# Turning the x tiles before they are combined, keys and values in turns, and a new order at the end of the key jobs, in a one-core gated cross-attention kernel

## The chip, the cores and the metric

The kernel runs on one core of a Trainium2 chip. The metric is the device time of one execution in microseconds, as the median of several runs. The core has five engines with a queue each: TensorE (PE in the profile; its weight loads are PEld), VectorE (DVE), ScalarE (ACT), GpSimd (POOL) and SyncE (SP), which here issues all the DMAs. Each engine works through its queue in order, and waits on semaphores for the others. The code fixes all five orders by hand.

## The reference, cut to what matters

```python
# x: (32, 64, 512), ctx: (32, 64, 512); 32 query heads, 8 key/value heads, 128 wide; float32
def xattn(x, ctx, mask, wq, wk, wv, wo):
    q = rope(heads(layernorm(x) @ wq))            # (b, 32, 64, 128)
    k = rope(repeat4(heads(ctx @ wk)))            # 8 heads, each used by 4 query heads
    v = repeat4(heads(ctx @ wv))
    attn = softmax(q @ k.T / sqrt(128) + mask)
    return merge(attn @ v) @ wo
x = x + tanh(g_xattn) * xattn(x, ctx, ...)
# then a mixture of 8 rank-16 experts, top 1, on layernorm(x)
logits = layernorm(x) @ route_w.T
x = x + tanh(g_ffn) * lora_of_the_best_expert(...)
```

Here rope(y) is y * cos + rotate_half(y) * sin.

## The kernel before, in words

**Precision.** A float32 product is made of three products of parts: each operand is split into a high part (the value rounded to fp32r by an ACT copy) and a low part (the value less the high part, a subtraction on DVE or POOL). So one product over 128 rows is three matmuls, and every tile that comes to PE has an ACT "high" and a DVE or POOL "low" first.

**Stages.** The 2048 tokens are 4 chunks of 512. The first stage is 64 *jobs* (list `JOBS`, L67): keys of a chunk are 8 jobs (one for each head), values of a chunk are 8 jobs. A job is 12 matmuls into one of four PSUM banks (score, turned, attn0, attn1, in turn; `make`, L767), so job n may start only when DVE has read the bank of job n - 4. Then come `WIDE` = 60 and 4 more *steps* (L1240 on for DVE): each does the scores, the softmax, the values and the output projection of a quarter chunk and the projection of later queries.

**What follows a key job.** ACT copies the two halves of the bank, swapped, to a rotation buffer (`shift`, L1434), POOL multiplies it by sin (`by_sin`, L1675), DVE multiplies the bank by cos into kst (`finish_job`, L1105, `by_cos`, L1095) and adds both (`finish_key`, L1120, `rope_add`, L1100). **After a value job** ACT makes the high part and DVE the low part, in vst. Queries are treated like keys: a sum of two products (`q_sum`, L1124), shift, by_sin, by_cos, rope_add. The rotation buffers are few (`rot_slot`, L234): two, or four while x_third is free for it, and a shift waits until its buffer's last user has been added.

**The x tiles.** The queries use a 2 x 2 block scheme with 7 products in place of 8. For that, sums and differences T1 to T4 of blocks of x are needed, as they are of wq. A *pair* is two tiles of 128 tokens, c0 and c1, of 512 columns each. There are 8 pairs, and `X_BESIDE` (L101) says beside which job each is worked on. Before: the tiles are normalised (DVE, with POOL's power for 1/std), then POOL makes T1 to T4 of both tiles (`combine_x`, L1657, 4 operations of 128 x 256, into `combined`), then PE turns c0's four blocks, the eight blocks of `combined` and two of c1's, 14 transposes of 128 x 128 into the three proj banks and small (`turn_x`, L785), and ACT and DVE split these banks into xB, high and low (`x_highs`, L1391, `x_lows`, L1085). The pairs lie at jobs 8, 11, 13, 16 and 32, 35, 38, 41; combined 1 job and turned 4 jobs after that. Three places in SBUF hold the x pairs.

**The end of the jobs.** From job 47 the first weights of wq are combined (`combine_weights`, L1636) and split, from job 50 the products of the first two query blocks stand between the key jobs (`Q_AFTER`), and after job 62 PE does the scores of step 0. The last rows of every engine's job loop then run into step 0, where PE turns the probabilities after `normalise(0)` on POOL, and multiplies them with the values after `prob_low(0)` on DVE.

The functions that the change touches, with what calls them, are:

## Time and profile before

| What | us |
|---|---|
| Median of 3 runs | 1132.73 |
| Lowest, highest | 1132.55, 1134.85 |
| Profiled execution, whole | 1134.35 |
| Its span in the profile | 1132.6 |
| PE busy in it | 1103.6 |
| DVE, ACT, POOL busy | 899.3, 630.8, 619.2 |
| TensorE clock granted, mean | 0.994 |

The span is the time from the first to the last instruction on the engines; the whole execution of the profile is 1.75 us more, and is itself inside the range of the three runs. In a timeline row the first number is the start in us from the start of the span, the second the time that the row covers, and the last, in square brackets, how long the engine had been idle and on whom it had waited. A matmul's shown time reaches past the start of the next one, so the time that a group of matmuls costs is read from one start to the next.

### The profile page before, as it was taken

How to read it: one execution, taken by the hardware profiler on the slowest of the kernel's cores; microseconds unless marked ns; L12 is line 12 of the kernel's file. 1: busy time of each engine (PE TensorE's matmuls, PEld its weight loads, DVE VectorE, ACT ScalarE, POOL GpSimd, SP SyncE). 2: the span in 40 equal slices, each digit the busy share in tenths (PEclk: the TensorE clock that was granted, in tenths of full speed). 3: DMA queues.
4: the chain of work that ended last, by engine and by line, in shares of the span. 5: the costliest groups of instructions: out<-in, count | busy, mean ns of one | idle time of the engine just before them, and what ended most of it. 6: DMA issues, size and time to landing. Idle time of an engine off the chain costs nothing.

```text
span 1132.6 us, 17085 instructions
## 1 busy us (share of the span) xinstructions
PE 1103.6 (97%) x5664; PEld 923.1 (82%) x5664; DVE 899.3 (79%) x1407; ACT 630.8 (56%) x1096; POOL 619.2 (55%) x519
## 2 busy tenths in 40 slices
PE   7999999989999999999999999999999999999998
PEld 6788888768888888888888778888888888888875
DVE  6975748877877878788778999877887888778887
ACT  6453446566666666666666545455555555555443
POOL 4751458868777777777764433343444443443423
PEclk9999999989999999999999999999999999999999
DMA  6869955476464646464559735453535353533201
GB/s 221 264 235 361 340 163 214 140 270 231 139 230 148 233 145 225 147 215 160 174 189 375 263 127 169 152 177 102 190 122 197 121 187 114 177 110 105 75 1 75
DMA packets 93510, 206.27 MB, mean 182 GB/s; under 512 B 8816, under 2 KB 41712, under 8 KB 87536
## 3 DMA queue, kind: packets, MB, share of 16 engines
q1 hardware_dynamic: 93424, 205.18, 53.3%
q8 instruction: 47, 0.77, 0.3%
q14 instruction: 39, 0.32, 0.1%
HBM read 122.31 MB, written 82.84 MB: 181 GB/s over the span
## 4 chain that ended last, share of the span: by engine, by line
PE 64%; DVE 14%; POOL 10%; issue 7%; ACT 4%; DMA 0%; DVEq 0%; SPq 0%; ACTq 0%; POOLq 0%
PE attn L896 20%; PE proj L830 17%; PE score L847 7%; PE attn L782 6%; POOL rot L1680 4%; PE score L782 3%; PE turned L782 3%; POOL wq_s L1655 2%; PE attn L881 2%; PE turned L858 2%; PE attn L883 2%; DVE q_r L1140 2%; DVE q_r L1098 1%; DVE row_sum L1169 1%; DVE wo_s L1093 1%
## 5 line engine op out<-in xcount | busy, mean ns | idle before, releaser
L896 PE MATMUL attn<-wo_s,o_s 128*128 128x512 f32 x1524 | 374.6, 395 | 0.8 <-DVE o_s L1189 0.8
L830 PE MATMUL proj<-xB,wq_s 128*128 128x512 f32 x1344 | 337.1, 394 | 4.2 <-ACT copies L1466 2.2
L896 PEld LDWEIGHTS attn<-wo_s,o_s 128*128 128x128 f32 x1524 | 280.9, 188 | 57.9 <-DVE o_s L1189 1.4
L830 PEld LDWEIGHTS proj<-xB,wq_s 128*128 128x128 f32 x1344 | 252.9, 189 | 58.5 <-ACT copies L1466 2.6
L1680 POOL TENSOR_TENSOR rot<-rot,tab 128x512 f32<-128x512 f32 x112 | 170.3, 1521 | 174.2 <-ACT rot L1445 174.0
L847 PEld LDWEIGHTS score<-k_r,q_r 128*128 128x128 f32 x1024 | 124.1, 193 | 13.6 <-DVE q_r L1103 8.0
L1444 ACT ACTIVATE rot<-q_r 64x512 f32<-64x512 f32 x86 | 54.2, 630 | 143.0 <-DVE q_r L1140 138.2
L847 PE MATMUL score<-k_r,q_r 128*128 128x64 f32 x1024 | 123.5, 274 | 3.2 <-DVE q_r L1103 3.2
L1181 DVE TENSOR_TENSOR p_low<-turned,p_high 64x512 fp32r<-64x512 f32 x128 | 88.0, 688 | 40.4 <-ACT p_high L1482 38.4
L1490 ACT ACTIVATE o_s<-attn 128x512 fp32r<-128x512 f32 x127 | 69.3, 595 | 77.6 <-PE attn L883 77.6
L1103 DVE TENSOR_TENSOR q_r<-q_r,rot 128x512 f32<-128x512 f32 x86 | 89.0, 1035 | 17.0 <-POOL rot L1680 11.8
L1680 POOL TENSOR_TENSOR rot_third<-rot_third,tab 128x512 f32<-128x512 f32 x40 | 61.5, 1539 | 68.4 <-ACT rot_third L1445 68.4
L1098 DVE TENSOR_TENSOR q_r<-q_r,tab 128x512 f32<-128x512 f32 x128 | 94.0, 734 | 4.7
L1201 DVE SCALAR_TENSOR_TENSOR acc<-attn,gates_t,acc 128x512 f32<-128x512 f32 x127 | 94.6, 745 | 3.4 <-PE attn L896 1.4
L1189 DVE TENSOR_TENSOR o_s<-attn,o_s 128x512 fp32r<-128x512 f32 x127 | 81.3, 680 | 5.4 <-ACT o_s L1490 5.4
L1140 DVE TENSOR_TENSOR q_r<-copies,proj 128x512 f32<-128x512 f32 x128 | 81.6, 674 | 0.0
L1481 ACT ACTIVATE p_high<-turned 64x512 fp32r<-64x512 f32 x128 | 75.4, 589 | 6.8 <-PE turned L858 4.4
L1482 ACT ACTIVATE p_high<-turned 64x512 fp32r<-64x512 f32 x128 | 75.9, 593 | 1.5
L1466 ACT ACTIVATE copies<-proj 128x512 f32<-128x512 f32 x96 | 57.4, 598 | 27.7 <-PE proj L830 26.3
L1692 POOL TENSOR_TENSOR prob_odd<-prob_odd,row_inv 128x512 f32<-128x512 f32 x32 | 43.5, 1359 | 51.3 <-DVE row_inv L1171 51.3
L1692 POOL TENSOR_TENSOR prob_even<-prob_even,row_inv 128x512 f32<-128x512 f32 x32 | 43.2, 1349 | 46.4 <-DVE row_inv L1171 46.4
L1444 ACT ACTIVATE rot_third<-q_r 64x512 f32<-64x512 f32 x40 | 25.2, 630 | 67.6 <-DVE q_r L1140 67.2
(230 smaller groups left out, 1702.7 us busy)
## 6 DMA issues: line engine op xcount, KB each, us to landing
wq_kept<-wq_s SPq DMA_DIRECT2D x16, 1792.0 KB, 6.3
wq_s<-wq_kept SPq DMA_DIRECT2D x16, 1792.0 KB, 8.4
v_kept<-vst SPq DMA_DIRECT2D x64, 256.0 KB, 4.7
v_s<-v_kept SPq DMA_DIRECT2D x128, 128.0 KB, 4.9
wo_kept<-wo_s SPq DMA_DIRECT2D x32, 512.0 KB, 3.7
wo_s<-wo_kept SPq DMA_DIRECT2D x32, 512.0 KB, 5.3
k_kept<-kst SPq DMA_DIRECT2D x32, 256.0 KB, 2.0
wq_raw<-in_wq SPq DMA_DIRECT2D x16, 512.0 KB, 5.5
```

Source lines behind the costliest of these rows:

```text
L782: last = e.matmul(b[:, :], stationary, moving, start=(kt == 0 and m == 0), stop=(kt == KT - 1 and m == 2))
L830: last = e.matmul(dst[:, :], wq_s[:, b % 2, A, s, kt, :], xB[:, B, mv, kt, :], start=(first and kt == 0 and m == 0), stop=(kt == 1 and m = ...
L847: last = e.matmul(score[:, col:col + SEQ], two_heads, k_r[:, u % 2, seq * SEQ:(seq + 1) * SEQ], start=True, stop=True)
L896: last = e.matmul(out_bank(k, bp)[:, :], o_s[:, s, bp, h, :], wo_s[n % WO_SLOTS][:, m, :], start=(h == 0 and i == 0), stop=(h == GROUP - 1 ...
L1098: e.tensor_tensor(dst, src, cos, ALU.mult).then_inc(times_cos, 1)
L1103: e.tensor_tensor(dst, dst, by_seq(rotated(r)), ALU.add).then_inc(rope_added, 1)
L1140: e.tensor_tensor(q_tile(b, j), by_seq(copies[:, copy, :]), by_seq(proj[PRODUCTS[i][2]][:, :]), ALU.add).then_inc(q_summed, 1)
L1181: e.tensor_tensor(p_low[rows, :, twin, :], turned[rows, :].rearrange("p (b n) -> p b n", b=PAIRS), p_high[rows, twin, :].bitcast(F32).rear ...
L1189: e.tensor_tensor(low, src, high.bitcast(F32), ALU.subtract).then_inc(out_low, 1)
L1201: e.scalar_tensor_tensor(out=acc[:, tile, :], in0=out_bank(k, bp)[:, :], scalar=gates_t[:, 0:1], in1=acc[:, tile, :], op0=ALU.mult, op1=AL ...
L1680: e.tensor_tensor(r3, r3, sin, ALU.mult).then_inc(times_sin, 1)
L1692: e.tensor_tensor(by_row(k), by_row(k), row_inv[:, k % 2, :].unsqueeze(2).to_broadcast([P, ROWS, SEQ]), ALU.mult).then_inc(normalised, 1)
```

## The change

It has three parts.

1. **x is turned first.** PE turns c0 and c1 as they are: 8 transposes into two banks, 3 jobs after the pair's place in `X_BESIDE`. ACT copies the two banks back over the tiles (`x_copies`, new). POOL combines these turned tiles, and ACT and DVE split c0, `combined` and c1 from SBUF into xB, 5 jobs after the place. There are five places for x pairs, two of them in `far_raw0`. The pairs lie at jobs 8, 11, 14, 18, 34, 36, 38, 40.
2. **Keys and values of chunk 1 in turns.** Jobs 16 to 31 alternate between a key and a value job.
3. **The end of the key jobs and the first steps.** On DVE the addition of a key (`finish_key`) moves behind the next job's query sums, or to where the next job begins; the row sums of step 0 come before the last key job is finished. On POOL the weights' last combine moves from step 0 to beside the end of the jobs, half of it between `subtract_max(0)` and `normalise(0)`; the zeros of p_low move behind `normalise(0)`. On ACT the copy of step 0's middle product goes ahead of the query's shift. The four rotation buffers last until job 62, where before they ended with job 59.

```diff
-JOBS = [*keys_of(0), *values_of(0), *keys_of(1), *values_of(1), *values_of(2), *values_of(3), *keys_of(3), *keys_of(2)]
+BOTH_1 = [job for pair in zip(keys_of(1), values_of(1)) for job in pair]
+JOBS = [*keys_of(0), *values_of(0), *BOTH_1, *values_of(2), *values_of(3), *keys_of(3), *keys_of(2)]
...
-X_BESIDE = {8: 4, 11: 5, 13: 6, 16: 7, 32: 0, 35: 1, 38: 2, 41: 3}
-X_COMBINE, X_TURN, X_PLACES = 1, 4, 3
+X_BESIDE = {8: 4, 11: 5, 14: 6, 18: 7, 34: 0, 36: 1, 38: 2, 40: 3}
+X_TURN, X_COMBINE, X_SPLIT = 3, 4, 5
...
-FOUR_UNTIL, ZEROS_BESIDE = 60, 62
+FOUR_UNTIL, ZEROS_BESIDE = 63, 63
...
             def turn_x(pair):
-                c0, c1 = (x_place(w) for w in X_PAIRS[pair])
-                T = combined[:, :, :, :].rearrange("p b k n -> p (b k n)")
                 e.wait_ge(ln_done, NORM_NO[X_PAIRS[pair][1]] + 1)
-                for i in range(4):
-                    b = (proj + [small])[i]
+                for c, w in enumerate(X_PAIRS[pair]):
                     if X_NO[pair]:
-                        e.wait_ge(x_low, 4 * X_NO[pair] - 4 + i + 1)
...
+                        e.wait_ge(x_copied, 2 * X_NO[pair] - 1 + c)
+                    turn(proj[c], 0, x_place(w), cols=KT).then_inc(x_turned, 1)
...
@@ vector, the loop over the jobs
                 if n in X_BESIDE:
                     x_norms_begin(X_BESIDE[n])
+                for q in SUMS_BESIDE.get(n, ()):
+                    q_sum(*q)
+                if n > KEYS_3_MADE:
+                    finish_key(JOBS[n - 1])
+                if n > SCORES_AFTER:
+                    sum_rows(0)
+                finish_job(n)
                 if n == SCORES_AFTER:
                     mask_scores(0)
-                for q in SUMS_BESIDE.get(n, ()):
-                    q_sum(*q)
-                finish_job(n)
...
-                finish_key(JOBS[n])
-                for w in SPLITS_BESIDE.get(n, ()) if n >= KEYS_3_MADE else ():
-                    raw_low(w)
+                if n < KEYS_3_MADE:
+                    finish_key(JOBS[n])
...
-                if n - X_TURN in X_BESIDE:
-                    x_lows(X_BESIDE[n - X_TURN])
-            sum_rows(0)
+                for w in SPLITS_BESIDE.get(n, ()) if n >= KEYS_3_MADE else ():
+                    raw_low(w)
+                if n - X_SPLIT in X_BESIDE:
+                    x_lows(X_BESIDE[n - X_SPLIT])
...
@@ vector, step 0, behind its early query sums
+                if k == 0:
+                    finish_key(JOBS[-1])
...
@@ scalar
+            def x_copies(pair):
+                for c, w in enumerate(X_PAIRS[pair]):
+                    e.wait_ge(x_turned, 2 * X_NO[pair] + c + 1)
+                    e.activation(x_place(w), proj[c][:, :], ACT.Copy).then_inc(x_copied, 1)
...
             def x_highs(pair):
+                e.wait_ge(x_copied, 2 * X_NO[pair] + 2)
                 for i, (src, (high, low)) in enumerate(x_split(pair)):
-                    e.wait_ge(x_turned, 4 * X_NO[pair] + i + 1)
+                    if i in (1, 2):
+                        e.wait_ge(x_combined, 4 * X_NO[pair] + 2 + i)
...
+                for p in middle if k == 0 else ():
+                    copy_product(*p)
                 for q in ropes[0]:
                     q_shift(*q)
-                for p in middle:
+                for p in middle if k else ():
                     copy_product(*p)
...
@@ gpsimd, combine_x
-                e.wait_ge(ln_done, NORM_NO[X_PAIRS[pair][1]] + 1)
+                e.wait_ge(x_copied, 2 * no + 2)
                 if no:
-                    e.wait_ge(x_turned, 4 * no - 1)
+                    e.wait_ge(x_low, 4 * no)
...
@@ gpsimd, the loop over the jobs
-                if n == SCORES_AFTER:
-                    subtract_max(0)
...
+                if n == SCORES_AFTER:
+                    subtract_max(0)
+                    combine_weights(HEAD_PAIRS + 1, (0,))
+                    normalise(0)
+                if n == ZEROS_BESIDE:
+                    e.wait_ge(rope_added, FOUR.stop)
+                    e.memset(p_low[:, :, :, :].bitcast(F32), 0.0).then_inc(zeros_set, 1)
-            normalise(0)
+            combine_weights(HEAD_PAIRS + 1, (1,))
```

The same in the instructions. On PE, from the values of chunk 0 to the first x pair (score, turned and attn are the banks of the jobs; tab holds the identity matrix of the transposes), before:

```order
L782 MATMUL attn<-wv_s,ctxT_52 128x512 x24
L782 MATMUL score<-wv_s,ctxT_52 128x512 x12
L754 MATMUL proj<-tab,x_near 128x128 x4
L754 MATMUL proj<-tab,combined 128x128 x8
L754 MATMUL small<-tab,x_near 128x128 x2
L782 MATMUL turned<-wv_s,ctxT_52 128x512 x12
```

and in the change:

```order
L793 MATMUL attn<-wv_s,ctxT_52 128x512 x24
L765 MATMUL proj<-tab,x_near 128x128 x8
L793 MATMUL score<-wv_s,ctxT_52 128x512 x12
L793 MATMUL turned<-wv_s,ctxT_52 128x512 x12
L793 MATMUL attn<-wv_s,ctxT_52 128x512 x12
```

The first pair's transposes move from behind job 12 to ahead of it, they are 8 and no longer 14, and none reads `combined`. The other seven pairs' blocks shrink in the same way.

On DVE, around the two query sums beside job 60 (q_r_71 and q_r_72 are query tiles, kst a key tile, wo_s a weight tile), before:

```order
L1103 TENSOR_TENSOR kst<-kst,x_third 128x512
L1093 TENSOR_TENSOR wo_s_61<-raw,wo_s_61 128x512
L1098 TENSOR_TENSOR kst<-attn,tab 128x512
L1103 TENSOR_TENSOR kst<-kst,rot 128x512
L1140 TENSOR_TENSOR q_r_71<-copies,proj 128x8x64
L1140 TENSOR_TENSOR q_r_72<-copies,proj 128x8x64
L1098 TENSOR_TENSOR kst<-score,tab 128x512
L1103 TENSOR_TENSOR kst<-kst,rot 128x512
L1093 TENSOR_TENSOR wo_s_62<-raw,wo_s_62 128x512
L1098 TENSOR_TENSOR q_r_71<-q_r_71,tab 128x8x64
L1098 TENSOR_TENSOR kst<-turned,tab 128x512
L1103 TENSOR_TENSOR q_r_71<-q_r_71,rot 128x8x64
```

and in the change:

```order
L1094 TENSOR_TENSOR wo_s_61<-raw,wo_s_61 128x512
L1104 TENSOR_TENSOR kst<-kst,x_third 128x512
L1099 TENSOR_TENSOR kst<-attn,tab 128x512
L1141 TENSOR_TENSOR q_r_71<-copies,proj 128x8x64
L1141 TENSOR_TENSOR q_r_72<-copies,proj 128x8x64
L1104 TENSOR_TENSOR kst<-kst,rot 128x512
L1099 TENSOR_TENSOR kst<-score,tab 128x512
L1099 TENSOR_TENSOR q_r_71<-q_r_71,tab 128x8x64
L1094 TENSOR_TENSOR wo_s_62<-raw,wo_s_62 128x512
L1104 TENSOR_TENSOR kst<-kst,rot 128x512
L1099 TENSOR_TENSOR kst<-turned,tab 128x512
```

One addition of a key is now behind the two query sums. Between these sums and the addition to q_r_71 there are as many instructions as before, and one more key addition among them.

On POOL, from the subtraction of step 0's maximum to the second step's (prob_even and prob_odd are the probabilities of steps 0 and 1), before:

```order
L1702 MEMSET p_low 128x1024
L1687 TENSOR_TENSOR prob_even<-prob_even,neg_max 128x512
L1680 TENSOR_TENSOR rot<-rot,tab 128x512 x2
L1692 TENSOR_TENSOR prob_even<-prob_even,row_inv 128x512
L1680 TENSOR_TENSOR rot<-rot,tab 128x512
L1655 TENSOR_TENSOR wq_s<-wq_raw,wq_s 128x2x256
L1655 TENSOR_TENSOR wq_s<-wq_raw,wq_s 128x256
L1680 TENSOR_TENSOR rot<-rot,tab 128x512
L1644 TENSOR_TENSOR combined<-wq_raw 128x256
L1645 TENSOR_TENSOR combined<-wq_raw 128x256
L1648 TENSOR_TENSOR combined<-combined,wq_raw 128x256
L1650 TENSOR_TENSOR combined<-wq_raw,combined 128x256
```

and in the change:

```order
L1705 TENSOR_TENSOR prob_even<-prob_even,neg_max 128x512
L1662 TENSOR_TENSOR combined<-wq_raw 128x256
L1663 TENSOR_TENSOR combined<-wq_raw 128x256
L1710 TENSOR_TENSOR prob_even<-prob_even,row_inv 128x512
L1698 TENSOR_TENSOR rot<-rot,tab 128x512
L1740 MEMSET p_low 128x1024
L1666 TENSOR_TENSOR combined<-combined,wq_raw 128x256
L1668 TENSOR_TENSOR combined<-wq_raw,combined 128x256
L1698 TENSOR_TENSOR rot<-rot,tab 128x512
L1673 TENSOR_TENSOR wq_s<-wq_raw,wq_s 128x2x256
```

The sine product of job 63 was ahead of the normalisation and is now behind it, with the zeros of p_low behind both. The four combines no longer stand ahead of the second step's subtraction.

## Rows read from the trace of the kernel before

**Rows 1.** The page, part 1: busy time (share of the span) xinstructions

```profile
PE 1103.6 (97%) x5664; PEld 923.1 (82%) x5664; DVE 899.3 (79%) x1407; ACT 630.8 (56%) x1096; POOL 619.2 (55%) x519
```

**Rows 2.** Stretches: us, busy of each engine, PEclk, DMA share, GB/s

```profile
210.00:240.00 30.00, 23.73 (x105) 18.92 (x104) 23.09 (x31) 17.00 (x30) 21.86 (x17) 0.83 0.68 225
```

**Rows 3.** PE's waits: engine, line <- releaser: us in total, times, longest us

```profile
PE proj L830 <- ACT copies L1466: 2.2, 1, 2.2
```

**Rows 4.** PE's timeline: start us, us, what, [idle before <- releaser]

```profile
42.22 2.43 PE L782 MATMUL score<-wv_s,ctxT 128*128 128x512 f32 x9
45.49 0.96 PE L782 MATMUL score<-wv_s,ctxT 128*128 128x512 f32 x3 [0.84 <-DVE wv_s L1093]
...
48.08 1.09 PE L754 MATMUL proj<-tab,combined 128*128 128x128 f32 x8 [1.20 <-POOL combined L1670]
...
49.14 3.00 PE L782 MATMUL turned<-wv_s,ctxT 128*128 128x512 f32 x12
...
57.87 1.04 PE L754 MATMUL proj<-tab,combined 128*128 128x128 f32 x8
58.74 0.38 PE L754 MATMUL small<-tab,x_near 128*128 128x128 f32 x2
```

**Rows 5.** DVE's timeline, the first x pair normalised

```profile
41.44 0.99 DVE L1073 TENSOR_SCALAR x_near<-x_near,moments,rstd 128x512 f32<-128x512 f32 x2
```

**Rows 6.** The transposes: count, duration in ns min/median/max, first and last start

```profile
L754 PE MATMUL proj<-tab,combined x64: 272/273/329, 48.1 to 149.7; 128*128 128x128 f32 x64
```

**Rows 7.** DVE's low parts of x in the same form

```profile
L1087 DVE TENSOR_TENSOR xB<-proj,xB x24: 675/680/684, 50.7 to 151.1; 128x512 fp32r<-128x512 f32 x24
```

**Rows 8.** Stretches in the x pairs' jobs, columns as in rows 2

```profile
60.00:80.00 20.00, 20.00 (x104) 16.93 (x103) 15.44 (x27) 10.94 (x21) 12.35 (x14) 1.00 0.64 221
...
110.00:140.00 30.00, 30.00 (x154) 25.37 (x153) 22.98 (x49) 11.49 (x23) 12.79 (x18) 1.00 1.06 351
```

**Rows 9.** POOL's timeline, the last combine of the first weights

```profile
152.51 0.73 POOL L1650 TENSOR_TENSOR combined<-wq_raw,combined 128x256 f32<-128x256 f32 x1
```

**Rows 10.** ACT's timeline, the first use of that

```profile
159.62 1.16 ACT L1433 ACTIVATE wq_s<-combined 128x512 fp32r<-128x512 f32 x2
```

**Rows 11.** PE's timeline from job 54 to step 1

```profile
199.00 1.52 PE L830 MATMUL proj<-xB,wq_s 128*128 128x512 f32 x6
200.35 2.88 PE L782 MATMUL attn<-ctxT,wk_s 128*128 128x512 f32 x12
...
213.25 2.40 PE L830 MATMUL proj<-xB,wq_s 128*128 128x512 f32 x6 [1.85 <-DVE q_r L1140]
215.45 3.78 PE L782 MATMUL attn<-ctxT,wk_s 128*128 128x512 f32 x12
219.76 2.00 PE L847 MATMUL score<-k_r,q_r 128*128 128x64 f32 x16 [0.53 <-DVE q_r L1103]
...
229.45 1.69 PE L830 MATMUL proj<-xB,wq_s 128*128 128x512 f32 x6 [2.15 <-ACT copies L1466]
232.87 1.11 PE L858 MATMUL turned<-tab,prob_even 128*128 128x128 f32 x4 [1.73 <-POOL prob_even L1692]
233.64 2.91 PE L830 MATMUL proj<-xB,wq_s 128*128 128x512 f32 x6
...
246.12 0.66 PE L858 MATMUL turned<-tab,prob_odd 128*128 128x128 f32 x4 [0.74 <-POOL prob_odd L1692]
```

**Rows 12.** DVE's timeline at the end of the jobs

```profile
201.64 1.77 DVE L1103 TENSOR_TENSOR kst<-kst,rot 128x512 f32<-128x512 f32 x1 [2.70 <-POOL rot L1680]
...
211.01 0.99 DVE L1103 TENSOR_TENSOR kst<-kst,rot 128x512 f32<-128x512 f32 x1
211.92 1.27 DVE L1140 TENSOR_TENSOR q_r<-copies,proj 128x512 f32<-128x512 f32 x2
...
218.53 1.18 DVE L1103 TENSOR_TENSOR q_r<-q_r,rot 128x512 f32<-128x512 f32 x1
```

**Rows 13.** POOL's timeline, the sine of job 63

```profile
228.86 1.28 POOL L1680 TENSOR_TENSOR rot<-rot,tab 128x512 f32<-128x512 f32 x1 [1.91 <-ACT rot L1445]
```

More of the change, by code:

```diff
@@ L371, in build @@
         acc_in = [sem(f"acc_in{t}") for t in range(HALF_TILES)]
[L372 removed]
+        x_in = [sem(f"x_in{i}") for i in range(max(X_PLACE) + 1)]
         first_in = [sem(f"first_in{i}") for i in range(len(FIRST))]
@@ L513, in x_split @@
             cols = slice(tt * P, (tt + 1) * P)
[L514 to L518 removed]
+            c0, c1 = (x_place(w) for w in X_PAIRS[pair])
+            for first, n, src in ((B11, 2, c0[:, :].rearrange("p (b k t) -> p b k t", b=2, k=2)),
+                                  (T1, 2, combined[:, 0:2]), (T3, 2, combined[:, 2:4]),
+                                  (B22, 1, c1[:, 2 * P:].rearrange("p (b k t) -> p b k t", b=1, k=2))):
+                yield src, [xB[:, first:first + n, part, :, cols] for part in range(2)]
         block = stack.enter_context(nc.Block())
```

64 lines of the change are left out of this document (28 added, 36 removed).

## The prediction

> **What bounds the kernel now.** I read the page's busy times first: PE is busy 1103.6 of 1132.6 us [rows 1], so a gain is either PE work removed or one of the few PE gaps closed. Then the stretches show where the gaps are. Up to 210 us PE is full but for its start and 45 to 49 us, from 250 us on it lacks some tenths of a us in 30, and 210 to 240 us is the exception: 23.73 us busy of 30, at a mean granted clock of 0.83 [rows 2]. The table of PE's waits says the same by cause; the largest one outside the start is that for ACT's copies [rows 3]. The timelines then give each gap its place: one of 0.84 and one of 1.20 us at the first x pair [rows 4], and 1.85, 0.53, 2.15, 1.73 and 0.74 us at the end of the key jobs, 7.0 us in sum [rows 11].
>
> What the clock adds there: six matmuls at full clock take 1.35 us from start to start, 199.00 to 200.35; at 213.25 they take 2.20 and the six at 233.64 are shown with 2.91 where 1.52 is usual. A key job of 2.88 is shown with 3.78 at 215.45 [rows 11]. That is 0.85 + 0.9 + 1.4 us, and 0.7 more for the scores that follow by their later end (an estimate): 3.9 us, at the lower of the two levels (1.2 GHz), behind idle gaps. So the stretch costs 10.9 us against full speed. Nothing else in the change's reach costs anything.
>
> **Part 1, x turned first.** Removed from PE: 14 - 8 = 6 transposes in each of 8 pairs, 48. Each is shown with 0.273 us [rows 6], but they overlap: eight of them take from 57.87 to 58.74, 0.109 each [rows 4]. 48 x 0.109 = 5.2 us. PE is the bound wherever seven of the eight blocks stand (20.00 of 20 and 30.00 of 30 us busy, rows 8), so all of it counts: 7 x 0.65 = 4.6 us for these seven.
>
> The first pair gives more. From the start of job 12 to that of job 13 PE takes 42.22 to 49.14, 6.92 us: it waits 0.84 for a wv part, and then 1.20 for POOL's last combine [rows 4]. Now the transposes come ahead of job 12 and wait only for the normalisation, which ends at 42.43 [rows 5]. They end 0.87 later, 43.3. Nine matmuls (2.04) bring PE to 45.35, the last three wait for the same wv part until 45.49, and end 0.68 later, 46.2 in place of 49.14: 3.0 us. Part 1 gives 4.6 + 3.0 = 7.6 us.
>
> What it adds: ACT copies two banks in each pair, 16 copies at 0.58 [rows 10], 9.3 us on an engine that is busy 10.94 of 20 us at its fullest here [rows 8]. POOL combines after these copies rather than before the transposes; nobody on PE waits for that now but through xB. DVE's low parts are as many, but with the source in SBUF. Before, from PSUM, all 24 large ones take 0.675 to 0.684 us [rows 7]. DVE operations with both inputs in SBUF take up to 1.77 us where POOL is working at the same time [rows 12]. So a low part costs 0 to 1.09 more. At all 24, and at half of that at the 8 small ones, this is 0 to 30.5 us of DVE time. I take a quarter, 8 us, since POOL's next combine waits for these very low parts and only the sines and 1/std meet them. It is hidden: DVE has 4.56 us free in 60 to 80 and 7.02 in 110 to 140 [rows 8], and PE has four banks, so DVE may be 4 jobs of 2.72 us late before PE feels it. If that cover is gone, each us of DVE is a us of PE.
>
> The Trainium skill (SBUF — State Buffer, "Who interferes with whom") states that a DVE instruction with two SBUF inputs contends with a GpSimd instruction that reads SBUF, that one with at most one SBUF input outside the two-port modes does not, and that the loser is fully blocked. By that rule the low parts of x lose a protection that the PSUM source gave them; the 1.77 against 0.68 us above agree with it. That is the rival of the slower side below.
>
> At the end of part 1, all 32 low parts must be there before POOL combines the first weights. Before, the last combine ended at 153.24 [rows 9], and ACT used it at 159.62 [rows 10]: 6.4 us to spare. Now the last x pair passes ACT (the value's high part, then four) and DVE first, about 2 us later (by 0.58 for an ACT operation). 4.4 us remain.
>
> **Part 2, keys and values in turns.** The PE work is the same. A key job leaves DVE two operations and POOL one, a value job one; in turns, the load on DVE is even. PE did not wait there before [rows 8], so nothing is gained: 0. It makes room for the 8 us above.
>
> **Part 3, the end of the key jobs.** All times here are on the old time axis, as if part 1 had gained nothing.
> - The 1.85 us gap before 213.25. The two sums at 211.92 no longer stand behind a key's addition (0.9 us, from 211.01), and DVE's idle 2.70 us before 201.64, in which it waited for POOL, is now used by what was behind [rows 12]. Between 0.6 us (everything contended) and 3.6 us. I take 1.8: the sums end at 211.3 rather than 213.1, and PE's gap is gone.
> - The scores at 219.76 wait for the addition that begins at 218.53 [rows 11, 12]. Between it and the sums DVE has seven instructions: two key additions, one query cosine, one weight's low part (0.68 to 1.77 each), two key cosines from PSUM (0.6), and itself 1.18. That is 5.1 to 9.5 us; between two and three of the four contended, as is usual for DVE here, makes 7.6, so 218.9. The scores gain 0.85 us. PE has finished job 62 at 215.5, so its wait there grows from 0.53 to 3.3 us: the 1.85 us has mostly moved.
> - The copy that PE waited for until 229.45 stood behind ACT's shift for job 63, and that behind the addition of a query. This addition now comes two instructions earlier. I take 1.5 us, between 0.5 and 3.
> - Values of step 0 at 238.7, right after the slow product of 233.64. The new chain is normalise, then on POOL the sine of job 63 (1.3) [rows 13], the key's addition on DVE (0.7), the shift on ACT into the same rotation buffer (two copies, 1.2), four high parts (2.4) [rows 10], the low parts and handing over (1.7). From a normalise that ends at 230.4 (before: 232.8, when PE turned the result, rows 11) this ends at 237.7. Gain 1.0 us; bounds 0 and 3.
> - The 0.74 us before 246.12 [rows 11] goes, as four combines no longer stand ahead of that step's subtraction.
>
> Of these only the last two reach the end, since each gap swallows the one before: 1.0 + 0.74 = 1.7 us. Slow clock is absorbed: PE is waiting anyhow in most of it. Bounds: 0, and 10.9 if all of the stretch came back.
>
> **Sum.** 7.6 + 1.7 = 9.3 us. The profiled execution took 1134.35 (span 1132.6); it would take 1125.1. The median of the runs shown is 1132.73, 1.6 lower, so 1123.4.
>
> The Trainium skill (TensorE: Matmul & The Clock Gate, Part 4) gives a PE transpose about 275 ns in a kernel's context. Our row agrees as a duration (0.273). Taken as the cost of each, 48 removed would give 13.1 us in place of 5.2 and a time near 1115.5; the distance between starts, 0.109, speaks against it.
>
> **Rivals.**
> - *A, the end comes back.* If DVE is rarely contended in part 3, the chain to the scores takes 5.1 us and the gaps mostly close, and with them the slow clock: 8 of 10.9 us, time 1132.7 - 7.6 - 8 = 1117. For it: DVE idles 2.70 us in front of the first gap. Against: POOL is busy nearly throughout there, and new waits on the same rotation buffer and bank remain.
> - *B, only the transposes count.* The wait at the first pair comes back in another place (DVE is full there) and part 3 gives nothing: 5.2 us, time 1127.5.
> - *C, slower.* Every low part of x meets POOL. 30.5 us more on DVE, half of it, 15.3, in the second four pairs; with the sines on POOL stretched and the next combine waiting for the low parts, nothing overlaps, and the free 7.02 us are not usable between them. The first weights come 15.3 + 2 us late against 6.4 us of slack: 10.9 at the first query product after job 49. The first four pairs would add theirs beyond 4 jobs, 15.3 - 10.9 = 4.4. That is 15.3 lost against 9.3 won, 1138.7. It turns slower once PE loses more than 9.3 us in both places. Against it: POOL is busy 12.79 of 30 us in 110 to 140 [rows 8], and mostly with the combines that exclude themselves.
> - That the change doesn't do what it says is no rival: the order of PE's instructions has 8 transposes in a block.
>
> **How the numbers follow.** Forecast 0.55, its own range 1121 to 1126 (part 3 from 0 to 4). A 0.23, B 0.14, C 0.05, and 0.03 for gaps in later steps that I don't see. The range reaches to A and over B: 1116 to 1128.5. About 0.2%, 2.3 us, is what can be told from no change. Faster: 0.91 (forecast, A, B nearly whole), same 0.04, slower 0.05.
>
> **What would show it.** Right: no PE idle before the first transposes beyond 0.3 us, job 13 starting near 46.2; the first query product 7.5 us earlier; blocks of 8 transposes taking 0.87 us; PE's longest new wait before the scores of step 0, on DVE's q_r; the wait at the second step's transposes gone. Wrong: xB low parts with a mean over 1.2 us; PE waits between 50 and 155 us; or a stretch behind job 60 without gaps and with a clock of 1.00, which is A.

## The result, and the profile after

| | before | after |
|---|---|---|
| Median of 6 runs each, us | 1133.79 | 1127.47 |
| Lowest, highest | 1132.43, 1138.88 | 1127.32, 1131.05 |
| Span of the profiled execution | 1132.6 | 1125.4 |

The ratio is 0.9947, with a 95% interval of 0.9923 to 0.997: the changed kernel is 6.0 us faster (3.4 to 8.7). The forecast was 9.3 us, to 1123.4, with 1121 to 1126 as its own range and 1116 to 1128.5 with the rivals. The direction and the wide range held, the forecast's own range did not: a third of the gain is missing.

The page of the changed kernel, part 1, answers to [rows 1]:

```profile
PE 1096.2 (97%) x5616; PEld 916.8 (81%) x5616; DVE 909.0 (81%) x1407; ACT 639.6 (57%) x1112; POOL 622.2 (55%) x519
```

PE has the 48 instructions less, DVE is 9.7 us busier (8 were forecast), ACT 8.8 (9.3 forecast). The 8 us stood for the low parts of x alone, and those cost 4.2 us (18.3 us of DVE before, 22.5 after), so that the sum on DVE is near by luck. The stretches (columns as in [rows 2]) answer to [rows 2] and [rows 8]:

```profile
210.00:240.00 30.00, 23.49 (x104) 19.52 (x103) 26.02 (x32) 15.89 (x29) 24.73 (x20) 0.83 0.82 281
60.00:80.00 20.00, 20.00 (x98) 16.77 (x97) 17.18 (x28) 12.24 (x24) 10.48 (x11) 1.00 0.71 228
110.00:140.00 30.00, 27.59 (x138) 22.70 (x137) 20.23 (x43) 11.76 (x22) 10.32 (x15) 1.00 1.07 366
```

Between 110 and 140 us PE was full before; now it lacks 2.41 us. That is one of the three signs of "wrong" that the prediction named. PE's timeline (columns as in [rows 4]) shows the first pair, the new waits, and the end, and answers to [rows 4] and [rows 11]:

```profile
41.65 1.09 PE L765 MATMUL proj<-tab,x_near 128*128 128x128 f32 x8
42.49 3.11 PE L793 MATMUL score<-wv_s,ctxT 128*128 128x512 f32 x12
45.44 2.88 PE L793 MATMUL turned<-wv_s,ctxT 128*128 128x512 f32 x12
...
89.40 3.06 PE L793 MATMUL score<-ctxT,wk_s 128*128 128x512 f32 x12 [0.28 <-DVE kst L1099]
...
125.34 1.06 PE L765 MATMUL proj<-tab,far_raw 128*128 128x128 f32 x8 [2.07 <-ACT far_raw L1401]
...
214.23 3.67 PE L848 MATMUL score<-k_r,q_r 128*128 128x64 f32 x16 [3.50 <-DVE q_r L1104]
...
226.39 1.65 PE L831 MATMUL proj<-xB,wq_s 128*128 128x512 f32 x6 [0.25 <-ACT copies L1480]
...
232.53 0.48 PE L882 MATMUL attn<-p_high,v_s 128*128 128x256 f32 x2 [2.76 <-issue]
...
233.69 4.34 PE L831 MATMUL proj<-xB,wq_s 128*128 128x512 f32 x12
```

The first pair is as forecast: no wait, job 13 at 45.44. The 1.85 us gap of [rows 11] is gone, and the scores of step 0 wait 3.50 us (3.3 forecast). New are the 2.07 us at the x turn beside job 39, and the 2.76 us ahead of the first values. The first query product starts at 158.55, 5.1 us earlier than before and not 7.5.

The table puts each kernel on one scale. A number is how much earlier than in the kernel before PE starts that piece of work, in us, in one profiled execution each. The start itself scatters (from -1.7 to 1.2 at job 8), so the differences from column to column count, the last two columns above all. Some of the profiled executions are slower than their kernel's median: that of e12 by 4.1 us, e5 by 2.8, e13 by 2.4, e3 by 2.3, e1 by 1.9, e2 by 1.1, the others by less than 1. Their rows are to be read with that in mind.

| | job 24 | job 32 | job 48 | scores 0 | values 0 | scores 2 | scores 5 | job 32 to 48 | job 48 to scores 5 |
|---|---|---|---|---|---|---|---|---|---|
| before starts at | 83.90 | 105.66 | 155.47 | 219.76 | 238.73 | 250.72 | 292.42 | | |
| after | 5.82 | 5.21 | 5.08 | 5.53 | 6.20 | 5.53 | 6.26 | -0.13 | 1.18 |
| e1_x_only | 5.44 | 4.86 | 1.57 | 1.58 | 3.20 | 0.39 | 1.10 | -3.29 | -0.47 |
| e2_end_only | 0.31 | 0.31 | 0.31 | 1.32 | 1.35 | 0.81 | 1.55 | 0.00 | 1.24 |
| e3_no_turns | 2.37 | -0.01 | -4.27 | -3.68 | -3.18 | -4.99 | -4.27 | -4.26 | 0.00 |
| e4_banks | 6.18 | 5.64 | 5.89 | 6.30 | 6.99 | 6.33 | 7.07 | 0.25 | 1.18 |
| e5_xb_early | 5.01 | 4.44 | -1.08 | -0.63 | -0.15 | -1.83 | -1.09 | -5.52 | -0.01 |
| e6_probs_first | 4.93 | 4.39 | 4.32 | 4.77 | 8.21 | 4.93 | 5.56 | -0.07 | 1.24 |
| e7_q_first | 5.52 | 4.97 | 4.07 | 6.19 | 4.85 | 4.36 | 5.11 | -0.90 | 1.04 |
| e9_six_more | 2.72 | 2.72 | 1.72 | 2.73 | 3.19 | 4.13 | 4.86 | -1.00 | 3.14 |
| e10_small_stores | 4.01 | 3.45 | 6.10 | 7.08 | 7.74 | 7.10 | 7.82 | 2.65 | 1.72 |
| e11_fetch_early | 5.26 | 4.68 | 6.50 | 6.96 | 7.41 | 5.53 | 6.26 | 1.82 | -0.24 |
| e12_wo_late | 3.22 | 2.68 | 1.15 | 3.80 | 3.60 | 1.98 | 2.72 | -1.53 | 1.57 |
| e13_all | 6.08 | 5.56 | 6.46 | 8.59 | 11.53 | 8.62 | 7.27 | 0.90 | 0.81 |

So the 6.26 us that the changed kernel is ahead at step 5 are 5.08 up to job 48 (0.84 of it a faster start, by chance), and 1.18 behind it. Part 1 gave 4.2 us in place of 7.6, part 3 gave 1.2 in place of 1.7. Of part 1, the 24 transposes of the second half should show as 2.6 us between jobs 32 and 48, and show as -0.13. That is the question of the experiments.

ACT's timeline says what stood ahead of the copies that PE waited for:

```profile
111.43 0.60 ACT L1472 ACTIVATE vst<-attn 128x512 fp32r<-128x512 f32 x1 [4.23 <-DMA v_kept<-vst]
...
117.33 0.60 ACT L1472 ACTIVATE vst<-attn 128x512 fp32r<-128x512 f32 x1 [4.77 <-DMA v_kept<-vst]
...
122.58 0.60 ACT L1472 ACTIVATE vst<-score 128x512 fp32r<-128x512 f32 x1 [4.14 <-DMA v_kept<-vst]
124.11 0.60 ACT L1472 ACTIVATE vst<-turned 128x512 fp32r<-128x512 f32 x1 [0.93 <-DMA v_kept<-vst]
124.60 1.08 ACT L1401 ACTIVATE far_raw<-proj 128x512 f32<-128x512 f32 x2
```

The two copies of the turn at 116.78 come at 124.60, and PE's next turn follows at 125.34. ACT cannot write a value job's high part until the store from that slot four value jobs ago has landed. Its waits for that, in 100 to 160 us, first the kernel before, then the changed one (us in total, times, longest):

```profile
ACT vst L1458 <- DMA v_kept<-vst: 7.6, 3, 2.6
```

```profile
ACT vst L1472 <- DMA v_kept<-vst: 18.8, 8, 4.8
```

Before, there were no copies of x, and PE stayed full beside 7.6 us of such waits. Now the next x turn waits for the copies that stand behind them.

### The profile page after: what moved, and what is told of

Same layout as the page of the kernel before. It is cut to its first block, busy times and chain, and to the rows that moved or that the text cites. A ratio compares the mean times of both kernels' runs of the same rounds, so it can differ in the third digit from the quotient of the medians.

```text
span 1125.4 us, 16990 instructions
## 1 busy us (share of the span) xinstructions
PE 1096.2 (97%) x5616; PEld 916.8 (81%) x5616; DVE 909.0 (81%) x1407; ACT 639.6 (57%) x1112; POOL 622.2 (55%) x519
## 4 chain that ended last, share of the span: by engine, by line
PE 61%; DVE 15%; POOL 10%; issue 7%; ACT 4%; SPq 2%; DMA 1%; DVEq 0%; ACTq 0%; POOLq 0%
PE attn L897 22%; PE proj L831 19%; PE score L848 8%; POOL rot L1698 3%; PE attn L793 2%; PE turned L859 2%; PE attn L882 2%; PE score L793 2%; PE attn L884 2%; POOL wq_s L1673 1%; DVE row_sum L1170 1%; DVE wo_s L1094 1%; DVE q_r L1141 1%; DVE o_s L1190 1%; DVE q_r L1099 1%
## 5 line engine op out<-in xcount | busy, mean ns | idle before, releaser
L1099 DVE TENSOR_TENSOR q_r<-q_r,tab 128x512 f32<-128x512 f32 x128 | 90.7, 709 | 6.2 <-ACT rot L1459 1.4
```

Of the source, the lines that this page charges most:

```text
L1099: e.tensor_tensor(dst, src, cos, ALU.mult).then_inc(times_cos, 1)
```

## Experiments

Each time is a median, with its distance from the median of the kernel before on the same chip (1132.70 to 1133.34), and the interval of the ratio to it. Between a variant and the changed kernel I compare these ratios, since the chips differ; 0.001 of them is 1.1 us.

### Parts 1 and 2 alone, and part 3 alone

e1_x_only is the changed kernel with the old order in the last key jobs and in step 0; for instance on DVE:

```diff
-                if n > KEYS_3_MADE:
-                    finish_key(JOBS[n - 1])
-                if n > SCORES_AFTER:
-                    sum_rows(0)
```

> The changed kernel with the old order of the last key jobs and first steps: parts 1 and 2 alone. Theory (part 1 gives some 4.2 us at job 48, because TensorE's second x turn of the second half waits 2.07 us for ScalarE's copies, and the rest of the gain is the end's): job 48 starts 4.2 to 5.1 us earlier than in the kernel before, and the kernel takes 4 to 5 us less than the kernel before. Rival (the two parts only work together, or what part 1 gains is given back at the old end, where other engines bound): under 2 us less. The forecast on record for part 1 alone was 7.6 us less.

Measured: 1131.39 us, -1.9 (0.9969 to 0.9988). e2_end_only is the reverse, the kernel before with the new end (the same lines added).

> The kernel before with part 3 alone (the new order of the last key jobs and first steps). Theory (the end of the jobs gains about 1 us between job 48 and step 4): 1 to 2 us less than the kernel before, with a wait of the first scores near 3.5 us for the rope of the query block and a slow clock after it. Rival (the whole difference behind job 48 is chance): no difference that can be measured.

Measured: 1131.52 us, -1.8 (0.9974 to 0.9991).

Part 3 is as forecast: 1.7 was the term, 1.24 is in the profile, 1.8 in the medians. Its wait of the scores is 3.27 us in e2 too. Parts 1 and 2 alone gave 1.9 us, the rival's number. Its second reason is at most a small part: 0.47 us are given back at the old end, and 3.29 are lost between jobs 32 and 48. The profile shows the same wait, longer:

```profile
127.77 1.65 PE L765 MATMUL proj<-tab,far_raw 128*128 128x128 f32 x8 [3.95 <-ACT far_raw L1395]
```

Up to job 50 the engines of e1 run the same instructions as those of the changed kernel; five kernels share that code (after, e1, e6, e7, e12), and from job 32 to 48 their profiles give -0.13, -3.29, -0.07, -0.90 and -1.53. So this wait is not a fixed price but one that scatters from run to run. The sum of the two parts, 3.7 us, falls short of the 6.0 of the whole. A scatter of up to 3 us in one place can hide that, and e1's profiled execution was its slowest; but its median is 1.9 us too, so the rival's first reason, that the parts work only together, is not excluded.

### What a transpose costs

e9_six_more adds to each pair:

```diff
+                turn(small, 0, x_place(X_PAIRS[pair][0]), cols=KT)
+                turn(small, 0, x_place(X_PAIRS[pair][1]), cols=2)
```

> The changed kernel with six more transposes for each of the eight pairs (48 in all, into a bank that nobody reads), which brings their number back to that of the kernel before. Theory (a transpose in a row of them costs the pitch of 0.109 us): 4.5 to 5.5 us more than the changed kernel, less 0 to 2 us that the waits at the turns absorb. Rival (0.27 us each, by the duration of one): some 13 us more. Other rival (these transposes lay beside waits and cost nothing): under 1.5 us more.

Measured: 1128.85 us, -4.5 (0.995 to 0.9976). The ratio of 0.9963 against 0.9947 makes it 1.8 us slower than the changed kernel (the intervals overlap), less than the 2.5 us that the theory allowed and far from the 13 of the first rival. Where PE is full the price is the forecast one: from job 8 to job 24 the changed kernel gains 4.98 us (5.82 - 0.84) and e9 2.46 (2.72 - 0.26), 2.52 us for 24 transposes, 0.105 each. PE's timeline shows six of them in front of the eight, 0.65 from start to start:

```profile
52.01 0.82 PE L765 MATMUL small<-tab,x_near 128*128 128x128 f32 x6
52.66 1.04 PE L765 MATMUL proj<-tab,x_near 128*128 128x128 f32 x8
```

In the second half the turn beside job 39 waits 0.80 us in place of 2.07, and for DVE's normalisation: 24 transposes cost 0.9 us there (-1.00 against -0.13), in a place that scatters by more than that. The duration of 0.27 us is not the price. The rest came back at the end, by the clock (below).

### Is it the dependence, or the DMA behind it?

e4_banks takes the dependence away, in part: pairs take the banks in turns.

```diff
-                    if X_NO[pair]:
-                        e.wait_ge(x_copied, 2 * X_NO[pair] - 1 + c)
-                    turn(proj[c], 0, x_place(w), cols=KT).then_inc(x_turned, 1)
+                    if X_NO[pair] >= 2:
+                        e.wait_ge(x_copied, 2 * X_NO[pair] - 3 + c)
+                    turn(x_bank(pair, c), 0, x_place(w), cols=KT).then_inc(x_turned, 1)
```

> The changed kernel with x turns of every other pair into the two other PSUM banks, so that a turn waits for the copies of the pair before the last one. Theory (the 2.07 us wait of the second half's second turn is TensorE's new dependence on ScalarE's copies): that wait is gone, job 48 starts about 2.3 us earlier than in the changed kernel, and the kernel takes 1.5 to 2.5 us less. Rival (the DMA queue is the bound of that stretch: the stores of values hold ScalarE, ScalarE holds TensorE's banks): a wait of like size appears at a later value job, and the time stays within 0.7 us of the changed kernel.

Measured: 1127.07 us, -6.3 (0.9931 to 0.9954), some 0.5 us under the changed kernel, which the intervals don't separate. PE no longer waits for ACT, but for DVE:

```profile
124.08 0.66 PE L768 MATMUL proj<-tab,far_raw 128*128 128x128 f32 x4 [1.22 <-DVE far_raw L1077]
...
137.73 0.66 PE L768 MATMUL proj<-tab,x_third 128*128 128x128 f32 x4 [0.75 <-DVE x_third L1077]
```

Only 0.85 us of the 2.07 is gone. The normalisation that it now waits for stands on DVE behind a value's low part, that waits for ACT's high part, and that for a store:

```profile
121.79 0.60 ACT L1475 ACTIVATE vst<-score 128x512 fp32r<-128x512 f32 x1 [4.14 <-DMA v_kept<-vst]
122.42 0.69 DVE L1122 TENSOR_TENSOR vst<-score,vst 128x512 fp32r<-128x512 f32 x1 [1.94 <-ACT vst L1475]
123.03 0.99 DVE L1077 TENSOR_SCALAR far_raw<-far_raw,moments,rstd 128x512 f32<-128x512 f32 x2
```

The theory was half right: the bank was the first of two roads from the stores to PE. How much the bank alone cost can't be told: from job 32 to 48 e4 is 0.38 us better than the changed kernel, within the scatter there.

e5_xb_early moves the big stores:

```diff
-XB_STORE = (24, 26, 28, 30, 32, 34, 36)
+XB_STORE = (24, 25, 26, 27, 28, 29, 30)
```

> The changed kernel with the seven stores of the split x (1 MB each) issued one a job at jobs 24 to 30 instead of one every other job at 24 to 36, so that they are out of the way of the stores of values at jobs 32 to 40. Theory (ScalarE's value highs wait for stores in a full DMA queue, and TensorE's turn waits for ScalarE: 2.07 us in the changed kernel, 3.95 us with parts 1 and 2 alone): ScalarE's waits for the DMA in 115 to 130 us fall from 9.8 us to under 3 us, TensorE's wait at the second turn of the second half falls under 0.7 us, job 48 starts 1.5 to 2 us earlier and the kernel takes 1 to 2.5 us less. Rival (the wait comes from ScalarE's and VectorE's order, not from the stores): the wait stays above 1.5 us and the time within 0.7 us of the changed kernel. A loss is possible if the stores now hold value jobs 24 to 31.

Measured: 1131.85 us, -1.5 (0.9967 to 0.9994), 4 us slower than the changed kernel. The gain that the theory expected became a loss, as the expectation held possible. ACT's waits became longer, and PE waits 4.66 us in one place:

```profile
111.81 0.60 ACT L1472 ACTIVATE vst<-turned 128x512 fp32r<-128x512 f32 x1 [6.55 <-DMA v_kept<-vst]
120.08 0.60 ACT L1472 ACTIVATE vst<-attn 128x512 fp32r<-128x512 f32 x1 [7.15 <-DMA v_kept<-vst]
126.00 0.60 ACT L1472 ACTIVATE vst<-attn 128x512 fp32r<-128x512 f32 x1 [4.80 <-DMA v_kept<-vst]
```

The DMA engines are all but full from the first of these stores on (share 0.88 in 89.6 to 95 us, 1.05 in 95 to 100), so a denser issue puts more megabytes ahead of each store of values. The big stores do bear on ACT's waits, and moving them without reducing them made it worse.

e10_small_stores and e11_fetch_early reduce the volume there. The first cuts the seven stores to [:, 0:256] of their 2048 columns, and the loads back (near 600 us) as well, so that it computes with a wrong x and serves for the time alone. The second:

```diff
-X_FETCH = [6, 8, 9, 14, 28, 29, 31, 33]
+X_FETCH = [6, 8, 9, 14, 28, 29, 17, 21]
```

> The changed kernel with the seven stores of the split x to the chip's memory, and their loads back for the second half, cut to an eighth (128 KB in place of 1 MB each), so that the second half computes with a wrong x: the run asks for time alone. Theory (the DMA engines are full from 88 us to 140 us, share 1.06 to 1.09, and every wait of TensorE between jobs 24 and 48 comes from that): the share in 100 to 130 us falls well below 1, ScalarE waits for no store of values, TensorE's 2.07 us wait is gone, and job 48 starts 2 to 3 us earlier than in the changed kernel. Rival (ScalarE's and VectorE's own order makes the wait): TensorE's wait stays above 1 us.

> The changed kernel with the x tiles of the last two pairs (1 MB in four loads) fetched at jobs 17 and 21, as soon as their places are free, in place of jobs 31 and 33: 1 MB less in the stretch in which the DMA engines are full (some 2.7 us of it at 388 GB/s). Theory (DMA volume in 88 to 140 us sets ScalarE's waits): the waits for stores of values shrink by 2 to 3 us, TensorE's wait of 2.07 us falls under 1 us, and the kernel takes 1 to 2.5 us less than the changed kernel. Rival (it is the order of the requests and not their volume): within 0.7 us of the changed kernel.

Measured: 1124.94 us, -8.1 (0.9907 to 0.9937), and 1126.63 us, -6.4 (0.9927 to 0.9955). ACT's waits for the stores in 100 to 160 us, e10 first, then e11:

```profile
ACT vst L1472 <- DMA v_kept<-vst: 1.8, 1, 1.8
```

```profile
ACT vst L1472 <- DMA v_kept<-vst: 14.0, 7, 4.8
```

In both PE's wait at job 39 is gone. In e10 the column from job 32 to 48 reads 2.65 us: the 24 transposes at their full forecast price (2.6). The stretches of e10, columns as before:

```profile
100.00:115.00 15.00, 15.00 (x68) 12.43 (x67) 9.73 (x19) 5.94 (x11) 2.39 (x3) 1.00 1.08 367
115.00:130.00 15.00, 15.00 (x76) 12.58 (x75) 11.99 (x26) 6.81 (x13) 5.28 (x8) 1.00 0.90 267
```

Both stand clear of the scatter of -0.07 to -3.29 in that column. So with less DMA volume between 88 and 140 us the new dependence costs PE nothing there, and with the full volume it costs 2.7 us. e10's share was expected to fall well below 1 and stayed at 1.08 in 100 to 115 us; the waits went even so. e11 gained 1.95 us on the changed kernel between jobs 32 and 48, but its ratio is only 0.7 us better, which is the rival's number: in its profile the clock at the end was low (below).

The volume is not the whole of it. The kernel before moved as much: in 88 to 140 us its DMA share is 1.05 at 355 GB/s, that of the changed kernel 1.03 at 361, and stores of values issued in 95 to 135 us land after 5.4 us in both (median). But in the changed kernel they are issued later. SyncE issues all transfers in order, and the first big store waits until the last low part of the first half's x is made, which part 1 has put off. DVE, then SyncE, in the changed kernel, and SyncE's wait in 60 to 92 us (us in total, times, longest):

```profile
88.33 0.41 DVE L1088 TENSOR_TENSOR xB<-x_near,xB 128x256 fp32r<-128x256 f32 x1
...
81.96 0.93 SPq L571 DMA_DIRECT2D v_kept<-vst  x2
88.77 0.33 SPq L654 DMA_DIRECT2D xB_kept<-xB  x1
```

```profile
SPq L654 <- DVE xB L1088: 5.9, 1, 5.9
```

Before, SyncE had no such wait. In 85 to 90 us the DMA share is now 0.11, where it was 0.81. The first big store is issued 10.7 us after PE starts the job that it stands beside (5.0 before), the last of the seven 13.6 us after (6.4 before), and the stores of values between them wait in the same queue. In e10 the first is 10.7 us late too, but the last only 4.0: with less volume SyncE catches up. The change also moves fetches here: the tiles of the second half's pairs were fetched at jobs 16, 18, 21 and 37, now at 28, 29, 31 and 33. And its pairs stand two jobs apart where they stood three. How the 2.7 us divide among the late queue, these fetches and the closer pairs no run shows; each of the other variants of the changed kernel keeps the late first store.

### Keys and values in turns

e3_no_turns:

```diff
-JOBS = [*keys_of(0), *values_of(0), *BOTH_1, *values_of(2), *values_of(3), *keys_of(3), *keys_of(2)]
+JOBS = [*keys_of(0), *values_of(0), *keys_of(1), *values_of(1), *values_of(2), *values_of(3), *keys_of(3), *keys_of(2)]
```

> The changed kernel with the second chunk's keys and values not in turns but eight keys, then eight values, as in the kernel before. Theory (part 2 by itself is worth nothing on TensorE's side, as the forecast on record had it): within 1 us of the changed kernel. Rival (the turns are what lets VectorE and GpSimd carry the x pairs beside key jobs): 1 to 3 us more, with waits of TensorE for times_cos or for a turn in jobs 16 to 24. Other rival (eight value jobs in a row now make more waits of ScalarE for the DMA ahead of job 32): a gap at jobs 24 to 32.

Measured: 1135.45 us, +2.1 (1.0009 to 1.0036): 8.6 us slower than the changed kernel, and slower than the kernel before. PE waits at three places where the changed kernel does not, and 1.94 us for DVE at the turn beside job 39, where that one waits 2.07 for ACT:

```profile
81.53 3.02 PE L793 MATMUL score<-wv_s,ctxT 128*128 128x512 f32 x12 [2.65 <-DVE kst L1099]
94.66 3.02 PE L793 MATMUL score<-wv_s,ctxT 128*128 128x512 f32 x12 [1.95 <-DVE vst L1119]
119.61 3.02 PE L793 MATMUL score<-wv_s,ctxT 128*128 128x512 f32 x12 [2.89 <-DVE vst L1119]
127.28 1.09 PE L765 MATMUL proj<-tab,far_raw 128*128 128x128 f32 x8 [1.94 <-DVE far_raw L1074]
```

In the first wait there is some of rival C. DVE's timeline of e3 ahead of it:

```profile
75.88 0.69 DVE L1104 TENSOR_TENSOR kst<-kst,rot 128x512 f32<-128x512 f32 x1 [2.10 <-POOL rot L1698]
...
77.09 3.45 DVE L1088 TENSOR_TENSOR xB<-combined,xB 128x512 fp32r<-128x512 f32 x2
...
80.80 0.68 DVE L1099 TENSOR_TENSOR kst<-score,tab 128x512 f32<-128x512 f32 x1
```

Two low parts of x take 3.45 us beside two sines of GpSimd, where the same two take 1.04 and 0.69 in the changed kernel: 1.7 us more, ahead of the operation that frees PE's bank at 80.80. DVE's wait of 2.10 us for a sine stands ahead of them. In the sum over all pairs the low parts barely differ. The changed kernel, then e3 (count, us in total, mean ns):

```profile
L1088 DVE TENSOR_TENSOR xB<-combined,xB 128x512 fp32r<-128x512 f32 x16 | 12.8, 820 | 2.2 <-ACT xB L1415 1.4
```

```profile
L1088 DVE TENSOR_TENSOR xB<-combined,xB 128x512 fp32r<-128x512 f32 x16 | 14.5, 931 | 2.0 <-ACT xB L1415 1.4
```

The two waits for vst come through ACT, which waits up to 8.00 us for a store with 24 value jobs in a row. The kernel before has the same order of jobs and none of these waits. Its low parts of x read PSUM, its fetches and big stores come earlier, and its SyncE is 4 to 6 us behind PE at the big stores, where e3's is 12 to 17; which of these does it, e3 does not separate. So part 2, priced at nothing, is what makes part 1 pay.

### The end of the key jobs

e6_probs_first, at step 0, on DVE (and likewise on ACT):

```diff
+                if k == 0:
+                    prob_low(k, 0, 1)
                 for q in ropes[0]:
                     q_cos(*q)
```

> The changed kernel with step 0's highs and lows of the turned probabilities ahead of the last rope of the first query block on ScalarE and VectorE. Theory (the 2.76 us wait ahead of values(0) is this order, and the slow clock after it follows from the wait): the wait falls to under 0.7 us, the clock stays at its upper level in the product after it, step 2 starts 2.5 to 4 us earlier than in the changed kernel and the time falls by 2.5 to 4 us. Rival (the moved rope is late for the scores of step 2, or something else holds values(0), such as the fetch of values): the gain is under 1 us.

e7_q_first, on DVE:

```diff
                     by_cos(ROPE_NO["q", *q], q_tile(*q), q_tile(*q))
+                    if n == 60:
+                        finish_key(JOBS[n])
+                        rope_add(ROPE_NO["q", *q], q_tile(*q))
```

> The changed kernel with the last rope add that the first scores need done on VectorE as soon as its sine and cosine are made (2.3 us earlier, ahead of a low part of wo and of the cosine of key job 61). Theory (the 3.5 us wait of the first scores and the slow clock behind it come from VectorE's order): the wait falls to about 1.2 us, the scores and key job 63 run less at 1.2 GHz (7.6 us for the two in the changed kernel, 4.9 at full clock), and values(0) starts 2 to 4 us earlier; the kernel takes 1 to 4 us less. Rival (the following chain of probabilities, not TensorE, sets values(0), or the slow clock moves elsewhere): scores earlier, but under 1 us of it left at step 2.

Measured: 1127.94 us, -5.4 (0.9926 to 0.9965), and 1128.30 us, -5.0 (0.9927 to 0.9966): no gain over the changed kernel, as the rivals had it. Each did its step and lost it at the next. First e6, then e7:

```profile
236.77 4.59 PE L897 MATMUL attn<-wo_s,o_s 128*128 128x512 f32 x12 [2.32 <-DVE o_s L1190]
```

```profile
213.57 2.00 PE L848 MATMUL score<-k_r,q_r 128*128 128x64 f32 x16 [1.86 <-DVE q_r L1104]
...
224.56 2.93 PE L831 MATMUL proj<-xB,wq_s 128*128 128x512 f32 x6 [3.45 <-ACT copies L1483]
```

In e6 values(0) starts with no wait, 2.0 us further ahead; then the moved rope stands in front of step 1's work on DVE, and 2.32 us come back with a product at low clock. In e7 the wait for the scores is 1.86 instead of 3.50, and 3.45 appear before the third product. DVE has no gap from 198.2 to 224.0 us in the changed kernel, so an order that serves one consumer earlier serves another later.

e12_wo_late is e7 with DVE work taken out of that stretch:

```diff
                 if k == 0:
+                    raw_low(("wo", 2))
                     finish_key(JOBS[-1])
+                    raw_low(("wo", 3))
```

> The kernel e7 (rope add of the first scores as early as it can be) with two low parts of wo (1.78 and 1.53 us) moved on VectorE from beside key jobs 60 and 62 into the gaps of 0.7 and 1.4 us that VectorE has in step 0. Theory (VectorE is busy without a gap from 199 to 224 us, so that reordering alone only moves TensorE's waits; work has to leave that stretch): the 3.45 us wait for the copies that e7 had falls under 1 us, scores(0) starts no later than there, and values(0) starts 2 to 4 us earlier than in the changed kernel; the kernel takes 1.5 to 4 us less. Rival (GpSimd's or ScalarE's chain holds the end as well): under 1 us less.

Measured: 1126.78 us, -6.2 (0.9928 to 0.9961). The 3.45 us wait fell to 0.25, and from job 48 to values(0) it is 2.45 us ahead (3.60 - 1.15) against 1.12 in the changed kernel. By scores(5) only 1.57 against 1.18 are left, since a product behind values(0) took 4.61 us where 2.90 is usual; but this profiled execution was the slowest of e12 by far. By the ratios e12 is 0.3 us under the changed kernel, the rival's number. The theory of the full DVE holds for the wait; the gain expected from it did not arrive.

### All together

e13_all is e4, e7, e11 and e12, with e6's order and its moved rope placed later:

```diff
                     sum_rows(k)
+                    for q in ropes_of(0)[0] if k == 1 else ():
+                        q_cos(*q)
+                        q_add(*q)
                     rest_of(k - 1)
```

> The changed kernel with what the runs so far point to: x tiles of the last two pairs fetched at jobs 17 and 21 (e11), x turns in alternating banks (e4), the first scores' rope add early (e7), two low parts of wo moved into step 0 (e12), and in step 0 the highs and lows of the probabilities first, with the first query block's last rope not in front of step 1's work as in e6 but behind its row sums. Theory (the stretch 88 to 140 us is bound by the DMA engines, and the end by VectorE's order and by the slow clock that each wait of TensorE brings): no wait over 1 us between jobs 24 and 48, the wait for values(0) under 0.7 us with no wait of 2.3 us behind it, and the clock at its upper level from there on: 1122 to 1125 us, 2.5 to 5.5 us under the changed kernel. Rival (each wait removed at the end comes back at the next engine, as in e6, e7 and e12): 1126 to 1127 us.

Measured: 1124.84 us, -7.9 (0.9907 to 0.9937), the fastest of the kernels that compute the whole. By the ratios it is 2.8 us under the changed kernel (the intervals just overlap). values(0) has no wait and comes 11.53 us earlier than before. Then it is given back in step 1, where the softmax is not ready:

```profile
236.36 0.66 PE L862 MATMUL turned<-tab,prob_odd 128*128 128x128 f32 x4 [2.45 <-POOL prob_odd L1724]
...
240.61 1.66 PE L834 MATMUL proj<-xB,wq_s 128*128 128x512 f32 x6 [0.83 <-DVE q_r L1144]
```

At scores(5) 7.27 us are left. The time is inside the theory's range, no wait between jobs 24 and 48 is over 1 us, and the granted clock is 1.00 from 225 to 250 us; but the wait of 2.3 us that was not to follow is there, with 2.45, and so the rival's mechanism took a part.

## Why the prediction was right in direction and too large

- **The first pair, 3.0 us: right.** Job 13 started 3.70 us earlier, 0.84 of it from the start: 2.86.
- **Seven blocks at 0.65, 4.6 us: the price right, the cover wrong.** e9 gives 0.105 us a transpose where 0.109 was read from [rows 4]. The first half got its gain: 5.82 - 0.84 = 4.98 from job 8 to job 24, against 3.0 + 3 x 0.65 = 4.95 forecast. The second half got none.
- **The step that failed** is the term "What it adds": the 9.3 us of ACT copies were priced at nothing, by ACT's busy time (10.94 of 20 us), and DVE, POOL and xB were followed but not PE's own next turn. It needs the bank that the copy empties, and on ACT the copy stands behind value jobs, which wait for stores. The sentence "nobody on PE waits for that now but through xB" is said of POOL's combines and holds for PE's order, but SyncE waits 5.9 us for xB's last low part, and the stores of values wait behind SyncE. [Rows 8] had a hint in their DMA share, 1.06, though PE was full beside it. Size: 3.4 us missing in part 1, of which PE's waits show 0.28 at job 28 (0.6 by the starts), 2.07 at job 39 and 0.34 at job 43. The 0.6 us at job 28 are there in e10 too and so not from the big stores: PE waits for a key's cosine on DVE, and that stands behind two low parts of x that take 2.38 us beside GpSimd.

```profile
86.02 2.38 DVE L1088 TENSOR_TENSOR xB<-combined,xB 128x512 fp32r<-128x512 f32 x2
...
88.66 0.68 DVE L1099 TENSOR_TENSOR kst<-score,tab 128x512 f32<-128x512 f32 x1
```

- **The 8 us on DVE: too large for what they stood for.** The low parts of x cost 4.2 us more, and all but the 0.6 us above was hidden.
- **Part 2 at 0: wrong.** It is worth 8.6 us once part 1 is in (e3). The reason given for it ("it makes room for the 8 us above") is right as far as that it makes room; two of e3's three new waits come from the stores and not from DVE's load. It should have been priced by taking it away.
- **Part 3, 1.7 us: right in sum.** The gap before the query product gone, the scores' wait 3.50 (3.3 forecast), values(0) 1.12 ahead (1.0), the wait at the second turn gone (0.74). "Slow clock is absorbed" is wrong: the twelve matmuls behind values(0) took 4.34 us where the kernel before has 2.90, 1.4 us on the path. Of the rest, 0.6 us came between scores(3) and scores(4), where the kernel before waits 0.20 us for a query and starts its scores 0.36 us late; e1 and e2 have the gain too, so it belongs to no one part, and I have no cause for it. The product in the kernel before:

```profile
239.75 2.90 PE L830 MATMUL proj<-xB,wq_s 128*128 128x512 f32 x12
```

- **The rivals.** A (the end comes back) did not happen: 23.49 us busy of 30 at a clock of 0.83, as before. B (1127.5) has the measured time by luck: the first pair's wait did not come back, and part 3 gave 1.2 us. C did not happen: the 16 low parts of `combined` have a mean of 0.82 us, under the 1.2 of the sign. Without part 2 (e3) it is 0.93, so that e3's loss is C's only in the 1.7 us of its first wait. The Trainium skill (SBUF — State Buffer, "Who interferes with whom") warned of it, and the 3.45 us for two low parts in e3 agree with it.
- **The Trainium skill's 275 ns a transpose** (TensorE: Matmul & The Clock Gate, Part 4) taken as a price would have made e9 13 us slower; it was 1.8.

## What to carry to other kernels

When work is moved to an engine with time to spare, look at what stands ahead of it in that engine's queue and what that waits for, not only at busy time. In this kernel a DMA share near 1 did no harm until PE came to depend on it. Look also at the queue that issues the transfers: here one store waited 5.9 us for its data, and all behind it in the queue waited with it. A part that "only makes room" must be priced by leaving it out beside the others. Where every helper engine is full, reordering moves a wait from one place to the next; look for work to take out or to spread.

## What the runs showed of the hardware

- The same wait of PE, 2.32 us ahead of values(0), left the granted clock at 1.00 in e9 (235 to 240 us), the upper of the two levels (2.4 GHz), while e11 had 0.55 in 230 to 235 and 0.76 in 235 to 240, a mixture with the lower (1.2 GHz). First e9, then e11:

```profile
235.54 0.48 PE L884 MATMUL attn<-p_high,v_s 128*128 128x256 f32 x2 [2.32 <-issue]
...
236.55 2.90 PE L833 MATMUL proj<-xB,wq_s 128*128 128x512 f32 x12
```

```profile
231.32 0.77 PE L882 MATMUL attn<-p_high,v_s 128*128 128x256 f32 x2 [2.32 <-issue]
```

  From values(0) to scores(2) the profiles took 11.05 us (e9), 12.66 (after) and 13.87 (e11) with the same work in the same order. So the length of a wait alone does not decide it, and up to 2.8 us of this kernel's end are in that. What does decide it these runs don't show.
- In 100 to 130 us a DMA share of 1.04 to 1.10 went with 365 to 400 GB/s, in the kernel before, the changed one, e4, e5 and e11, whose order of transfers differs. In e3 a store of values held ACT for up to 8.00 us.
